# Routed rows four apart in memory, pages in four lanes: a top-2 expert layer at the end of a fused model

## What is computed

```python
B, NTOK, D = 128, 96, 64             # 12288 tokens of width 64
logits = xf @ Wr + br                # 64 experts
topk_logits, topk_idx = jax.lax.top_k(logits, 2)
gates = jax.nn.softmax(topk_logits, axis=1)
combine = jnp.zeros((T, E)).at[jnp.arange(T)[:, None], topk_idx].add(gates)
for e in range(64):
    h = jax.nn.relu(xf @ W1[e] + b1[e])      # 64 -> 128
    y = h @ W2[e] + b2[e]                    # 128 -> 64
    out = out + combine[:, e:e + 1] * y
```

## Time and profile before

| what | value |
|---|---|
| median of three runs | 2484.33 us (2482.07 to 2492.51) |
| the profiled execution's own time | 2486.96 us |
| its span, first to last instruction | 2485.1 us |
| routing stage, first to last scatter issued | 1728.5 to 2024.1 us |
| expert stage, first transposes to last result scatter | 2029.3 to 2457.3 us |
| granted TensorE clock in both stages | 0.50 |
| busy over the span: PE, DVE, ACT, POOL | 74%, 67%, 45%, 43% |

### The profile page before, as it was taken

The page is one execution under the profiler, slowest core; times in us unless marked ns, Lnnn a source line. Parts: engine busy times, 40 slices in busy tenths (PEclk is TensorE's granted clock), DMA queues, the critical chain, the costliest instruction groups (busy, mean ns, idle before and its releaser), DMA issues.

```text
span 2485.1 us, 55409 instructions
## 1 busy us (share of the span) xinstructions
PE 1843.3 (74%) x17723; PEld 1432.8 (58%) x17723; DVE 1667.6 (67%) x5137; ACT 1113.8 (45%) x3614; POOL 1062.9 (43%) x846
## 2 busy tenths in 40 slices
PE   5888887999999999999997477774333336666662
PEld 2367775777777777777775255553212225555551
DVE  0067773588888888888886699996888843333334
ACT  2477762344444444444443398873212123444340
POOL 0056650134344444434433222212777755445553
PEclk9889996899999999999996588876555555555555
DMA  9910000000000000000000000005000031111114
GB/s 289 279 45 0 0 1 1 2 2 2 1 0 0 0 0 0 0 0 0 0 0 1 0 1 1 1 0 190 22 22 21 22 93 36 35 35 37 36 29 163
DMA packets 79641, 84.93 MB, mean 34 GB/s; under 512 B 53792, under 2 KB 68256, under 8 KB 78240
## 3 DMA queue, kind: packets, MB, share of 16 engines
q1 hardware_dynamic: 66064, 66.50, 9.5%
q0 software_dynamic: 13312, 13.85, 1.7%
q10 hardware_dynamic: 144, 3.15, 0.3%
HBM read 55.78 MB, written 27.69 MB: 34 GB/s over the span
## 4 chain that ended last, share of the span: by engine, by line
PE 34%; DVE 22%; issue 18%; POOL 14%; DMA 4%; another core or an unknown queue 4%; ACT 3%; DVEq 1%; POOLq 0%; SPq 0%; ACTq 0%
POOL routed_rows L1488 8%; PE PS L698 5%; PE PS L992 5%; DMA arena<-in_x_dram 4%; PE PS L665 3%; PE PS L732 3%; POOL rstd L1389 3%; PE PS L713 3%; PE PS L1002 2%; DVE XR L1642 2%; DVE XR L1842 2%; DVE XR L1638 1%; PE PS L747 1%; PE PS L772 1%
## 5 line engine op out<-in xcount | busy, mean ns | idle before, releaser
L1112 ACT ACTIVATE arena<-PS 128x384 f32<-128x384 f32 (+2 forms) x376 | 162.7, 451 | 342.6 <-remote 147.6
L1501 POOL DMA_INDIRECT expert_rows<-arena x224 | 215.3, 961 | 217.9 <-DVE arena L2044 155.8
L1638 DVE TENSOR_REDUCE XR<-PS 128x2 f32<-128x192 f32 (+2 forms) x768 | 173.8, 280 | 104.7 <-PE PS L698 104.7
L1488 POOL DMA_INDIRECT routed_rows<-XR,SLu x192 | 208.9, 1088 | 81.1 <-issue 77.8
L2024 DVE TENSOR_TENSOR arena<-PS,XR 128x512 f32<-128x512 f32 x56 | 38.7, 692 | 295.9 <-PE PS L992 199.5
L698 PE MATMUL PS<-arena 32*128 32x96 f32 (+2 forms) x3072 | 234.3, 285 | 0.0
L992 PE MATMUL PS<-arena,XR 64*128 64x64 f32 x896 | 148.8, 410 | 89.8 <-issue 89.0
L698 PEld LDWEIGHTS PS<-arena 32*128 32x128 f32 x3072 | 198.5, 192 | 20.6
L1359 ACT ACTIVATE XR<-arena 128x257 f32 x448 | 153.3, 407 | 111.3 <-issue 90.7
L1148 ACT ACTIVATE XR<-PS 128x256 f32<-128x256 f32 x512 | 167.2, 381 | 67.3 <-PE PS L713 67.1
L1434 POOL TENSOR_TENSOR arena<-arena,mhalf 96x16 f32<-96x16 f32 x32 | 93.3, 2914 | 241.6 <-DVE arena L1684 241.6
(11 more groups left out here) (309 smaller groups left out, 4693.8 us busy)
## 6 DMA issues: line engine op xcount, KB each, us to landing
arena<-in_x_dram SPq DMA_DIRECT2D x32, 784.0 KB, 10.5
arena<-in_t_experts_dram SPq DMA_DIRECT2D x8, 1028.0 KB, 12.3
routed_rows<-zt SPq DMA_DIRECT2D x14, 528.0 KB, 5.8
arena<-routed_rows SPq DMA_DIRECT2D x56, 132.0 KB
expert_rows<-arena POOLq DMA_INDIRECT x224
WP<-in_t_pack_dram SPq DMA_DIRECT2D x1, 3428.5 KB, 20.4
mixed_rows<-Hb SPq DMA_DIRECT2D x4, 768.0 KB
routed_rows<-XR,SLu POOLq DMA_INDIRECT x192
```

What stands on the lines that cost most here:

```text
L1112: return act.activation(dst, src, ACT.Identity, **kw)
L1488: pool.indirect_dma_start(XD, bass.IndirectOffsetOnAxis(SLu[:, u, k, b:b + 1], 0), XG[:, u, b, k, :], None).then_inc(scat[u], 16)
L1501: pool.indirect_dma_start(YD, bass.IndirectOffsetOnAxis(yi[:, u % 4, k:k + 1], 0), yb[:, u % 4, k, :], None).then_inc(e_st[u % 2], 16)
L1638: dve.tensor_reduce(negmax[:, p, j, :], PS[:, S_:S_ + 2, S_AT[j]:S_AT[j] + QB * (j + 1)], AX_X, ALU.max, negate=True).then_inc(b_max, 1)
```

## The change

The rows of a lane, a quarter of the slots (LANE = 7168), are written four apart: slot s lies in row 4 * (s mod 7168) + s // 7168. So a load of 512 consecutive rows gives partition p the four rows 4p to 4p+3, one from each lane, as one run of 1056 bytes instead of four runs of 264 bytes. A group then holds pages 2g and 2g+1 of each of the four lanes. Three things follow in the code: the load's pattern, the slot arithmetic in `d_places` (the cast to integers becomes four operations more, the last of which writes the integers), and the order in which the page numbers are packed into `blku`.

```diff
+LANE = NBLK * SLOT // KB
...
+        lane = sb("lane", [P, 2, 2 * NV])
...
-                sp.dma_start(xb[:, u, :, :], XD[ds(g * (EB * SLOT), EB * SLOT)].rearrange("(k p) d -> p k d", p=P)
+                sp.dma_start(xb[:, u, :, :], XD[ds(g * (EB * SLOT), EB * SLOT)].rearrange("(p k) d -> p k d", p=P)
...
-                        four = act.value_load(blku[0:1, ds(g * (EB // PACK) + k // PACK, 1)], min_val=0, max_val=NX ** PACK - 1)
+                        four = act.value_load(blku[0:1, ds(g + k // PACK * (NBLK // EB), 1)], min_val=0, max_val=NX ** PACK - 1)
...
-                link = Link(dve, chain6, g, 14)
+                link = Link(dve, chain6, g, 15)
...
                 dve.wait_ge(d_exp, g + 1)
+                dve.tensor_scalar(lane[:, 0, :], TS_[:, :], float(LANE), None, ALU.is_ge)
                 link(dve.tensor_scalar(gsum[:, :], gde[:, u, 1, :], 1.0, None, ALU.add))
+                dve.scalar_tensor_tensor(lane[:, 1, :], TS_[:, :], 2.0 * LANE, lane[:, 0, :], ALU.is_ge, ALU.add)
                 link(dve.reciprocal(one, gsum[:, :]))
+                dve.tensor_scalar(lane[:, 0, :], TS_[:, :], float(KB), None, ALU.mult)
+                link(dve.scalar_tensor_tensor(lane[:, 1, :], TS_[:, :], 3.0 * LANE, lane[:, 1, :], ALU.is_ge, ALU.add))
                 dve.tensor_tensor(two, gde[:, u, 1, :], one, ALU.mult)
-                dve.tensor_copy(SLu[:, u, :, :].rearrange("p k b -> p (k b)"), TS_[:, :]).then_inc(d_slots, 1)
+                dve.scalar_tensor_tensor(SLu[:, u, :, :].rearrange("p k b -> p (k b)"), lane[:, 1, :], 1.0 - KB * LANE, lane[:, 0, :],
+                                         ALU.mult, ALU.add).then_inc(d_slots, 1)
...
-            page = PS[0:1, 6, 0:NBLK].rearrange("p (n j) -> p j n", j=PACK)
-            link(dve.tensor_copy(bpk[0:1, 1, :], page[:, 3, :]))
+            page = PS[0:1, 6, 0:NBLK].rearrange("p (w k n h) -> p k h w n", w=2, k=2, h=2)
+            b0, b1, b2 = (t.rearrange("p (w n) -> p w n", w=2) for t in (bpk[0:1, 0, :], bpk[0:1, 1, :], blku[:, :]))
+            link(dve.tensor_copy(b1, page[:, 1, 1]))
```

More of the change, by code:

```diff
@@ L2011, in _ @@
             dve.wait_ge(d_blkp, 1)
-            page = PS[0:1, 6, 0:NBLK].rearrange("p (n j) -> p j n", j=PACK)
-            link(dve.tensor_copy(bpk[0:1, 1, :], page[:, 3, :]))
-            link(dve.scalar_tensor_tensor(bpk[0:1, 0, :], bpk[0:1, 1, :], float(NX), page[:, 2, :], ALU.mult, ALU.add))
-            link(dve.scalar_tensor_tensor(bpk[0:1, 1, :], bpk[0:1, 0, :], float(NX), page[:, 1, :], ALU.mult, ALU.add))
-            dve.scalar_tensor_tensor(blku[:, :], bpk[0:1, 1, :], float(NX), page[:, 0, :], ALU.mult, ALU.add).then_inc(d_blk, 1)
+            page = PS[0:1, 6, 0:NBLK].rearrange("p (w k n h) -> p k h w n", w=2, k=2, h=2)
+            b0, b1, b2 = (t.rearrange("p (w n) -> p w n", w=2) for t in (bpk[0:1, 0, :], bpk[0:1, 1, :], blku[:, :]))
+            link(dve.tensor_copy(b1, page[:, 1, 1]))
+            link(dve.scalar_tensor_tensor(b0, b1, float(NX), page[:, 1, 0], ALU.mult, ALU.add))
+            link(dve.scalar_tensor_tensor(b1, b0, float(NX), page[:, 0, 1], ALU.mult, ALU.add))
+            dve.scalar_tensor_tensor(b2, b1, float(NX), page[:, 0, 0], ALU.mult, ALU.add).then_inc(d_blk, 1)
             dve.wait_ge(d_rows, NR)
@@ L2034, in e_out @@
                 link = Link(dve, chain6, g, 2)
-                link.base += 2 * NR + 14 * NR
+                link.base += 2 * NR + 15 * NR
                 for h in range(2):
```

## The result

The changed kernel takes 2488.7 us, the median of 20 runs (2479.61 to 2497.89), against 2479.33 us for the kernel before, 20 runs on the same chip (2470.96 to 2492.51). The ratio is 1.0036 with a 95% interval of 1.0022 to 1.0050: slower by 0.36%, about 8.9 us, with 5.5 to 12.4 us as the interval, and within the 0.5% that I had set as the bound of no change. My +6.4 us lies inside that interval, so the time alone can't tell it from the measured size; the traces can.

What follows compares the result with a forecast made beforehand. The prediction took the DVE-POOL loop of the routing stage as the bound there. Slot arithmetic +6.7 us and first load -0.3 us gave +6.4 us, an expected median of 2490.7 us, range 2480 to 2499 for 8 in 10.

Steps and rivals of the forecast that it cites:

- My +6.4 us: Whole kernel: predicted net slowdown, +6.7 us for slot arithmetic less 0.3 us for the first load.
- What bounds the kernel: Routing stage: DVE and POOL wait for each other in a closed loop, so DVE's piece up to SLu counts fully.
- Slot arithmetic, 0.42 us a step: Routing stage, DVE: added operations lengthen each of 16 steps by 0.42 us, +6.7 us; bounds +2.4 and +14.1 us.
- The forecast of 2490.7 us: Whole kernel: expected median, 0.26% slower, from the 2484.33 us median of the runs shown; chance 0.69.
- 3 x 0.09 + 0.22 = 0.49: DVE's slot chain, per step: three additions in a neighbour's shadow at 0.09 us, a fourth with a new link at 0.22.
- -0.07: DVE's write of SLu, per step: the last operation takes 0.17 us where the replaced cast averaged 238 ns.
- The rule on the pipe that has to empty: DVE's slot chain: by the skill page each addition takes its whole 0.17 us, 9.8 us in all; the forecast rejected it.
- The loads: Expert stage: only the first load is on the path, 0.3 us shorter; 1056-byte packets at 42 ns, later loads hidden.
- The scatters, page numbers and lanes, 0: Scatters into routed_rows, page packing and result scatters: no change, 0 us; bounds for the routed_rows scatters -1 and +1 us.
- The faster one: Expert stage: small load packets cause the slow stretches, so long runs gain over 0.5%, 2472 us; chance 0.09.
- POOL hides it: Routing stage: POOL is the bound and hides the added DVE work; 2484 us if all were hidden; chance 0.06.
- The slower one: Routing stage: each small operation costs a full chained step and POOL's scatters stretch; +14 us, 2498 us; chance 0.16.

Runs made afterwards that it cites:

- the experiment above: Changed kernel with its slots-times-four operation as a scalar_tensor_tensor instead of a tensor_scalar; ratio to the kernel before 1.0015 [0.9997, 1.0033], 19.25 us a step.
- the arithmetic alone: Kernel before plus the four added DVE operations and chained wait, coefficients leaving slots unchanged, loads and rows as before; ratio 1.0031 [1.0008, 1.0054].
- the loads alone: Kernel before with only the load pattern changed to 1056-byte runs; ratio 0.9986 on a chip without slow stretches, 1.0003 on one with them.
- two kernels in the same order: Kernel before and changed layout, both with gates moved ahead of d_norm and SLu written right after the slot sum; side by side 0.9974 (old layout), 0.9964 (new).

## Why the prediction was right, and where its sizes were off

**What bounds the kernel.** Right. The loop of DVE and POOL took over every added operation, and DVE's wait for the power stayed at 1.71 to 1.92 us.

**Slot arithmetic, 0.42 us a step.** The mechanism held, the size was too small: 0.55, so +8.8 us instead of +6.7. The forecast of 2490.7 us stands only 2.0 us above the measured 2488.7, and that is partly luck: the three runs that I started from had a median 5.0 us above that of the twenty (2484.33 against 2479.33), which made up for a loss put too small. The pair of steps that ends at 1904.21 can be taken apart. It lasts 39.07 us (L1937 at 1865.14 and 1904.21) against 38.02 (L1935 at 1868.12 and 1906.14), +0.525 a step.

- From the start of the first of the chain to that of the write DVE took 0.52 us and takes 1.00 and 1.15 in turn, +0.555. I had 3 x 0.09 + 0.22 = 0.49. With L2005 unstretched, in the experiment above, it takes 1.02 and 0.96, so +0.47: the prices by start distances were right, and what I left out is that L2005 would be stretched. I had given the stretch away together with the cast, as if it belonged to that one instruction. It was not every second cast either, but the six that started late enough in a scatter; their mean of 238 ns was read rightly.
- From the write to POOL's first scatter: 1.25 and 1.00 us before, 1.07 and 1.01 after, -0.085. I had -0.07.
- POOL's third scatter: 1.49 and 1.62 us before, 1.59 and 1.64 after, +0.06. I had nothing for it. DVE's bf16 product starts 0.69 and 0.83 us into it before, 0.79 and 0.84 after, and the scatter's end moves with the product. The rows of before for it:

```profile
1882.74 1.49 POOL L1488 DMA_INDIRECT routed_rows<-XR,SLu  x1 [0.31 <-issue]
1883.43 0.36 DVE L1957 TENSOR_TENSOR arena<-arena 128x384 bf16<-128x384 bf16 x1
...
1901.44 1.62 POOL L1488 DMA_INDIRECT routed_rows<-XR,SLu  x1 [0.30 <-issue]
1902.27 0.36 DVE L1957 TENSOR_TENSOR arena<-arena 128x384 bf16<-128x384 bf16 x1
```

Together +0.53, which is this pair within the rounding of the rows.

**The rule on the pipe that has to empty.** By the Trainium skill (VectorE: DVE Perf Modes, The DRAIN you can't avoid) the sum was 9.8 us, as an estimate, and the measured 8.8 is nearer to that than my 6.7. The rows do not bear out what I took from it, though: L2002 starts 0.08 us behind L2001, which lasts 0.17, while chained operations, for which a semaphore was to cost nothing extra, start 0.22 us or more behind. I had read the section too narrowly: it adds that an operation that is not held starts earlier. The sum came close by way of the stretch. With another kind of operation and the same number of them it shrank to 0.45 us a step.

**The loads.** First load: 0.3 us less, as put. It repeats: 2.04, 2.09, 2.10 and 2.05 us in four traces with long runs, 2.35, 2.34, 2.42 and 2.28 in four without, all with slow stretches. The average packet was mis-sized: 6.9% of 16 x 356 us over 6904 packets is 57 ns, not 42, so a load takes some 0.46 us on sixteen engines instead of 0.33. That is an average; 47 loads make 6016 of the 6904 packets. Both are well below one group's time, and none of it was waited for, before or after. The Trainium skill's section on runs of at least 512 bytes (DMA: Bandwidth & Descriptors, Specifications) is borne out by the rate, 16.5 bytes a ns instead of 12.3 by the queue's own bytes and time (6.49 MB in 6.9%, 6.36 MB in 9.1%); it says nothing on whether anyone waits for that rate.

**The scatters, page numbers and lanes, 0.** Right within what the runs tell: with the arithmetic alone the step is 19.34 us, with the layout as well 19.35.

**The rivals.** The faster one needed 0.995 or less and is refuted by the loads alone on a chip with slow stretches (1.0003 [0.9981, 1.0026]). "POOL hides it" is refuted by the gap of 1.10 to 1.17 us that ends with DVE's write. The slower one needed 0.78 us a step; its mechanism, stretching, is real but gave only about 0.15 us of the step (0.555 - 0.47 on DVE, 0.06 on POOL).

**What stays open.** The traces show when the engines hold each other: a cast or `tensor_scalar` that starts 0.54 us or more into a scatter lasts until just before the scatter's end, and the third scatter lasts until some 0.44 us after the end of a bf16 product that starts in it. What the two engines share there, and why a `scalar_tensor_tensor` is spared, no run shows. What holds PE back in the slow stretches: the kernels only show that it is not the loads.

## What to carry to other kernels

When two engines wait for each other in turn, each instruction between a wait and the result that the other one needs costs its full step, so first move what the result does not need out of that piece, and only then argue about cheaper arithmetic. A stretch belongs to the place and the kind of an instruction: if you remove a stretched one, look where its successor starts within the other engine's operation, and price it as stretched if it is of the same kind and starts as late. The same look pays on the other side: between two kernels in the same order, a product that no longer started within POOL's third scatter went with a step 0.54 us shorter, as much as the whole slot arithmetic cost. Better DMA descriptors buy nothing where the ring of loads is already ahead, however much their own rate improves.

## What the runs showed of the hardware that I had not expected

The same program takes 2350 us on one chip and 2480 on the others used. The traces put the difference in the expert stage, with the granted clock at 0.50 in its middle on both; what differs between the chips, or in how the program lay on them, is open. The result scatters of the kernel with the arithmetic alone, on the fast chip:

```profile
L1502 POOL DMA_INDIRECT expert_rows<-arena x224: 954/958/1079, 2041.9 to 2325.4; - x112
```

That is 283.5 us, against 412 to 417 us elsewhere. POOL runs its scatters there back to back, as the timeline shows (0.96 us each and 0.30 between them):

```profile
2100.06 0.96 POOL L1502 DMA_INDIRECT expert_rows<-arena  x1 [0.30 <-issue]
2101.32 0.96 POOL L1502 DMA_INDIRECT expert_rows<-arena  x1 [0.30 <-issue]
```

And PE in a slow stretch of the changed kernel, on a chip that has them:

```profile
2202.32 0.38 PE L983 MATMUL PS<-WP,arena 64*64 64x64 f32 x2 [0.89 <-issue]
2203.04 0.36 PE L983 MATMUL PS<-WP,arena 64*64 64x64 f32 x1 [0.33 <-issue]
2203.75 0.92 PE L983 MATMUL PS<-WP,arena 64*64 64x64 f32 x12 [0.35 <-issue]
```

Single products start some 0.72 us apart with no engine named as what they wait for, and then twelve run together. A forecast of 0.4% on this kernel is therefore only good against the kernel before on the same chip: the chips differ by more than ten times as much.
